# Packing 0/1 rows as byte pairs, an even split of the last rows, and a shared accumulator for the two halves of layer 0

## The reference

```python
# layer 0: keep only edges between nodes of one class, average, mix with h0
a0 = adj * (y @ y.T)
a0 = a0 / maximum(sum(abs(a0), axis=1), 1e-12)
x = layernorm(x + 0.9 * (a0 @ x) + 0.1 * h0)
# layer 1: tanh of the adjacency's own square (one value where there is an edge)
filt = tanh(adj * adj) * (adj > 0)          # then the 350 largest of a row are kept
h2 = tanh(x @ W_proj + b_proj)
x = layernorm(x + relu(filt @ (h2 @ W_gcn) + b_gcn))
```

## Time and profile before

| | |
|---|---|
| median of 3 runs | 467.92 us |
| the profiled execution | 467.66 us |
| its span, from the first to the last instruction | 465.9 us |
| mean granted TensorE clock | 0.986 |
| PE, DVE, ACT, POOL busy | 94%, 81%, 57%, 35% of the span |
| layer 0 with its last blocks | to about 289 us |

### The profile page before, as it was taken

The page is one execution under the profiler, slowest core; times in us unless marked ns, Lnnn a source line. Parts: engine busy times, 40 slices in busy tenths (PEclk is TensorE's granted clock), DMA queues, the critical chain, the costliest instruction groups (busy, mean ns, idle before and its releaser), DMA issues.

```text
span 465.9 us, 15131 instructions
## 1 busy us (share of the span) xinstructions
PE 438.7 (94%) x5104; PEld 386.3 (83%) x5104; DVE 377.9 (81%) x1359; ACT 263.5 (57%) x355; POOL 161.5 (35%) x310
## 2 busy tenths in 40 slices
PE   3659999999999999999999999999999999999994
PEld 2448898888888988888888887888888888888883
DVE  5988999999999999999999976675575575575562
ACT  4997998999999999999999934900000000000000
POOL 3022543455444455554445541221211211211222
PEclk9977999999999999999999999999999999999998
DMA  8999999999999999999999200000000000000000
GB/s 262 411 414 420 419 417 417 415 408 411 409 422 420 422 423 420 424 423 412 417 419 422 60 2 1 13 11 17 17 11 17 17 11 17 17 11 17 17 11 23
DMA packets 25518, 108.50 MB, mean 233 GB/s; under 512 B 5097, under 2 KB 15490, under 8 KB 15490
## 3 DMA queue, kind: packets, MB, share of 16 engines
q1 hardware_dynamic: 25490, 108.14, 57.5%
HBM read 105.57 MB, written 2.56 MB: 232 GB/s over the span
## 4 chain that ended last, share of the span: by engine, by line
PE 75%; DVE 10%; ACT 5%; issue 5%; DMA 2%; POOL 2%; POOLq 0%; DVEq 0%; ACTq 0%; SPq 0%
PE acc L521 64%; PE words L471 6%; DVE a_bits L783 3%; DMA a_rows<-in_adj_dram 2%; PE feat_acc L584 2%; PE proj_acc L595 2%; ACT count_out L685 2%; DVE turned L870 2%; PE xnt_acc L576 1%; ACT count_out L678 1%; ACT x_parts L664 1%; POOL xs L438 1%; ACT count_out L754 1%; DVE z_high L921 1%; ACT count_out L746 1%
## 5 line engine op out<-in xcount | busy, mean ns | idle before, releaser
L521 PE MATMUL acc<-x_parts,turned 128*128 128x257 f16 (+1 forms) x1600 | 195.2, 276 | 3.2 <-DVE turned L870 1.0
L678 ACT ACTIVATE count_out<-a_rows,ones 128x2688 bf16<-128x2688 f32 (+1 forms) x80 | 190.2, 2377 | 0.5 <-DMA a_rows<-in_adj_dram 0.2
L521 PEld LDWEIGHTS acc<-x_parts,turned 128*128 128x128 fp8e4 (+1 forms) x1600 | 154.4, 98 | 28.9 <-issue 3.8
L521 PE MATMUL acc<-f_parts,turned 128*128 128x256 f16 (+1 forms) x1560 | 171.6, 273 | 0.8 <-DVE turned L870 0.8
L521 PEld LDWEIGHTS acc<-f_parts,turned 128*128 128x128 fp8e4 (+1 forms) x1560 | 152.0, 98 | 19.3 <-issue 1.3
L783 DVE TENSOR_SCALAR a_bits<-a_rows 128x2688 bf16<-128x2688 f32 (+1 forms) x80 | 116.7, 1459 | 2.7 <-DMA a_rows<-in_adj_dram 2.3
L421 POOL TENSOR_TENSOR var_eps<-mean_var,consts 128x1 f32<-128x1 f32 x80 | 18.6, 232 | 266.1 <-DVE mean_var L1077 139.7
L870 DVE TENSOR_SCALAR turned<-a_words 128x320 uint16 (+1 forms) x305 | 66.9, 233 | 53.2 <-PE acc L521 52.8
L424 POOL TENSOR_TENSOR rstd<-var_eps,consts 128x1 f32<-128x1 f32 x80 | 86.5, 1081 | 6.3
L870 DVE TENSOR_SCALAR turned<-same_class 128x320 uint16<-128x320 uint16 x313 | 71.3, 254 | 0.1
L471 PEld LDWEIGHTS words<-pack,a_bits 128*128 128x128 bf16 (+1 forms) x1600 | 51.3, 97 | 9.7 <-DVE a_bits L783 7.8
(11 more groups left out here) (111 smaller groups left out, 288.3 us busy)
## 6 DMA issues: line engine op xcount, KB each, us to landing
a_rows<-in_adj_dram SPq DMA_DIRECT2D x39, 1344.0 KB, 7.8
a_rows<-in_adj_dram SPq DMA_DIRECT2D x39, 1156.0 KB, 8.3
out_dram<-xn SPq DMA_DIRECT2D x39, 64.0 KB, 1.5
h_rows<-in_L_gnn_h_dram SPq DMA_DIRECT2D x19, 128.0 KB, 8.1
xs<-in_x_dram SPq DMA_DIRECT2D x3, 640.0 KB, 10.0
xs<-in_x_dram SPq DMA_DIRECT2D x1, 512.0 KB, 10.3
y_nat<-in_L_gnn_y_dram SPq DMA_DIRECT2D x1, 304.0 KB, 3.6
a_rows<-in_adj_dram SPq DMA_DIRECT2D x1, 84.0 KB
```

What stands on the lines that cost most here:

```text
L521: mm = pe.matmul(acc[par][0:m, 0:cols], bits, parts[:, b, 0:cols], start=first and b == blocks[0], stop=last and b == blocks[-1])
L678: act.activation(count_out[0:m, 0:w], a_rows[par][h][0:m, 0:w], ACT.Relu, bias=ones[0:m, 0:1], scale=-HUGE, accum_out=col).then_inc(s_coun ...
```

## The change

Three things are changed together.

- A block's cast writes bytes, 0x3C for a zero and 0x3D for a one. Two neighbouring bytes are read as one f16 weight, whose value is linear in both bits. A packing product so covers 128 pairs of columns: 20 products of 17 columns (16 of powers of two up to 128, one for the count) in place of 40 of 9. ACT takes the offset away and scales by 1024 (`Relu` with a bias), after which a 16-bit word holds 8 rows of two columns. `unpack` makes 8 instructions of 320 elements as before, and `multiply_blocks` reads its weights at every second byte.
- The rows are cut into 38 full blocks and two of 68 rows (the even and the odd rows of the last 136). All loads by pairs begin at row 0 and the halves are 2560 and 2440 columns wide. The words of the two short blocks are copied by three instructions each.
- In layer 0 the product of 257 columns becomes one of 128 (high half) and one of 129 (low half and ones) with the same weights, both added into the same 128 columns of `acc`; `add_high` and `add_low` become one `add_rows`.

The labels' packing at the start follows the new layout (10 turns become 5, 50 products of 256 columns become 25 of 512), and the last check weighs rows differently, in one more instruction. The diff, cut:

```diff
-BITS = 16
+BITS = 8
...
-    FULL = N // P
-    TAIL = N - FULL * P
-    NB = FULL + 1
+    FULL = N // (2 * P) * 2
+    TAIL = (N - FULL * P) // 2
+    NB = FULL + 2
+    COLS = NB // 2
...
+        if isinstance(b, int) and b >= FULL:
+            return a[FULL * P:N, cols].rearrange("(p e) c -> e p c", e=2)[par]
+        v = a[0:FULL * P, cols].rearrange("(s p e) c -> e s p c", p=P, e=2)[par]
...
-        a_bits = [sb(f"a_bits{h}", [P, HB * P], BF16) for h in range(2)]
+        a_bits = [sb(f"a_bits{h}", [P, HB * P], U8) for h in range(2)]
...
-                for b in range(h * HB, HB if h == 0 else NB):
-                    c, d = column(b) - HALF[h].start, spacing(b)
+                for b in range(h * HC, h * HC + HC):
+                    c = (b - h * HC) * P
                     mm = pe.matmul(words[par][:, b * PITCH:b * PITCH + WORDS + 1],
-                                   a_bits[h][0:m, c:c + (P - 1) * d + 1:d], pack[0:m, :], start=True, stop=True)
+                                   a_bits[h][0:m, :].bitcast(F16)[:, c:c + P], pack[0:m, :], start=True, stop=True)
...
             def multiply_blocks(n, par, m, parts, blocks, first=False, last=False):
-                cols = PARTS if parts is x_parts else 2 * F
                 for b in blocks:
-                    bits = turned_at(n, par)[:, b, :].bitcast(F8)[:, 0:m]
-                    mm = pe.matmul(acc[par][0:m, 0:cols], bits, parts[:, b, 0:cols],
-                                   start=first and b == blocks[0], stop=last and b == blocks[-1])
+                    bits = turned_at(n, par)[:, b // 2, :].bitcast(F8)[:, b % 2:2 * m:2]
+                    begin, end = first and b == blocks[0], last and b == blocks[-1]
+                    if parts is f_parts:
+                        mm = pe.matmul(acc[par][0:m, 0:2 * F], bits, parts[:, b, :], start=begin, stop=end)
+                    else:
+                        if not begin:
+                            pe.matmul(acc[par][0:m, 0:F], bits, parts[:, b, 0:F], start=False, stop=False)
+                        mm = pe.matmul(acc[par][0:m, 0:F + 1], bits, parts[:, b, F:PARTS], start=begin, stop=end)
+                        if begin:
+                            pe.matmul(acc[par][0:m, 0:F], bits, parts[:, b, 0:F], start=False, stop=False)
...
+                        act.activation(to[:, :, 0:WORDS + 1], of[:, :, 0:WORDS + 1], ACT.Relu, bias=less_full, scale=UNIT)\
+                            .then_inc(s_words, 1)
...
-                dve.tensor_scalar(a_bits[h][0:m, 0:w], a_rows[par][h][0:m, 0:w], 1.0, None,
-                                  ALU.is_equal).then_inc(s_bits, 1)
+                dve.tensor_scalar(a_bits[h][0:m, 0:w], a_rows[par][h][0:m, 0:w], 1.0, float(ZERO_BYTE),
+                                  ALU.is_equal, ALU.add).then_inc(s_bits, 1)
...
-            def add_high(n, par, m):
+            def add_rows(n, par, m):
                 dve.wait_ge(s_inverse, n + 1)
                 dve.wait_ge(s_xh, n + 1)
-                dve.scalar_tensor_tensor(z_high[0:m, :], acc[par][0:m, 0:F], rs[0:m, 1:2],
-                                         xh[par][0:m, :], ALU.mult, ALU.add).then_inc(s_zhigh, 1)
-
-            def add_low(n, par, m):
-                dve.wait_ge(s_zhigh, n + 1)
                 if not isinstance(n, int) or n >= 2:
                     dve.wait_ge(s_xn, n - 1)
-                dve.scalar_tensor_tensor(z[par][0:m, :], acc[par][0:m, F:2 * F], rs[0:m, 1:2],
-                                         z_high[0:m, :], ALU.mult, ALU.add).then_inc(s_z, 1)
+                dve.scalar_tensor_tensor(z[par][0:m, :], acc[par][0:m, 0:F], rs[0:m, 1:2],
+                                         xh[par][0:m, :], ALU.mult, ALU.add).then_inc(s_z, 1)
```

More of the change, by code:

```diff
@@ L77, in rows_in, with steps @@
     def rows_in(a, b, par, pair, cols):
[L79 to L83, removed]
-        if isinstance(b, int):
[L85 to L99, removed]
+        if isinstance(b, int) and b >= FULL:
+            return a[FULL * P:N, cols].rearrange("(p e) c -> e p c", e=2)[par]
+        v = a[0:FULL * P, cols].rearrange("(s p e) c -> e s p c", p=P, e=2)[par]
+        if isinstance(b, int):
+            return v[pair]
+        return v[bass.ds(pair, 1), :, :].rearrange("a p c -> p (a c)")
+    def steps(eng, step, lag, after={}, first=4):
+        first = max(first, lag + 2 + lag % 2)
         for t in range(first):
@@ L103, in steps @@
                 after[t]()
-        with eng.Fori((first - 1) // 2, (FULL - 1) // 2) as i:
+        with eng.Fori(first // 2, FULL // 2) as i:
+            step(i * 2, 0, i)
             step(i * 2 + 1, 1, i)
-            step(i * 2 + 2, 0, i + 1)
         for t in range(FULL, NB + lag):
@@ L121, in steps4 @@
             step(t, t % 2, t // 2, 0, t)
-        count = (FULL - first) // 4
-        with eng.Fori(0, count) as i:
+        with eng.Fori(0, (FULL - first) // 4) as i:
             for c in range(first, first + 4):
                 step(i * 4 + c, c % 2, i * 2 + c // 2, i, c)
-        for t in range(first + count * 4, NB + lag):
+        assert (FULL - first) % 4 == 0 and first % 2 == 0
+        for t in range(FULL, NB + lag):
             step(t, t % 2, t // 2, 0, t)
@@ L222, in packed_path @@
         GRAM_W = PART * WORDS
[L223 removed]
+        GRAMS = TILES
         EARLY_GRAMS = 3 * GRAMS
@@ new lines, in _ @@
+            pool.affine_select(out=pack[:, WORDS:WORDS + 1], in_=pack[:, WORDS:WORDS + 1],
+                               compare_op=ALU.not_equal, fill=1.0, base=-(P - 1), pattern=[[-1, 1]],
+                               channel_multiplier=1).then_inc(s_pack, 1)
+            for bit in range(BITS):
+                pool.wait_ge(s_pack, bit + 3)
+                pool.affine_select(out=pack[:, 0:WORDS], in_=pack[:, 0:WORDS], compare_op=ALU.not_equal,
+                                   fill=float(1 << bit), base=-bit * WORDS, pattern=[[-1, WORDS]],
+                                   channel_multiplier=1).then_inc(s_pack, 1)
@@ L397, in _, with zeros_as_words @@
+            def zeros_as_words(rows):
+                return -ZERO_VALUE * sum(1 << bit for bit in range(BITS) if rows > bit)
+            whole, rest = divmod(TAIL, WORDS)
+            for c, v in ((less_full, zeros_as_words(BITS)), (less_long, zeros_as_words(whole + 1)),
+                         (less_short, zeros_as_words(whole)), (less_count, -ZERO_VALUE * 2 * TAIL)):
+                pool.memset(c, v).then_inc(s_const, 1)
             pool.memset(ident[:, :], 0.0).then_inc(s_const, 1)
-            for c, v in ((neg_half, -0.5), (ln_eps, LN_EPS), (alpha, ALPHA)):
+            for c, v in ((neg_half, -0.5), (ln_eps, LN_EPS), (alpha, ALPHA), (row_weight, 2.0)):
@@ L865, in unpack @@
                     dve.wait_ge(s_acc, n - 1)
-                last = HALF_BITS if m == P else 1
-                for bit in range(lo // 2, min(hi // 2, last)):
+                last = -(-m // WORDS)
+                for bit in range(lo, min(hi, last)):
                     shift = ONE_BIT - bit
```

266 lines of the change are left out of this document (129 added, 137 removed).

## The result

The changed kernel takes 483.94 us (median of 4 runs, 483.25 to 489.14) where the kernel before takes 467.86 (467.48 to 468.11): a ratio of 1.0368, with a 95% interval of 1.0296 to 1.0441. It is slower, by 16.1 us. The prediction said 481.3 us, within 476 to 491. The profiled execution took 483.54 us with a span of 481.7, 15.8 longer than before. The highest of the four, 489.14 us, had a mean granted clock of 0.964 where the other three had 0.971; it has no trace, so what made it longer is open. It widens the interval.

A forecast was written before the change was run, and what follows sets the result against it. PE and DMA were taken as equally long in layer 0, with DMA's end deciding. Later drain 11.5, clock 2.1 and checks -0.2 sum to +13.4 us on the median 467.92: 481.3 us, range 476 to 491.

The forecast's parts named there:

- The engines of 68 rows: Row loads of the last two blocks: 68 rows use four DMA engines, the same four for both, 12.9 us a block.
- The last landing: 278.6 us: End of layer 0's row loads: 25.7 us for both short blocks from 252.9, where the kernel before cast at 267.08.
- After the last landing: End of layer 0: 2.24 us of DVE work, then 10.7 us for the last two blocks' products, ending at 291.6.
- The clock: 2.1 us, bounds 0 and 5: PE, idle while late rows come, drops to the low clock for some 4.3 us of products, losing 2.1 us.
- PE's step, 6.20 - 0.49 + 0.21 = 5.92 us: PE in a layer 0 step: packing saves 0.49 us, the split product adds 0.21, leaving it under DMA's 6.21.
- The split term 0.21: Layer 0 product on PE: a pair of 128-column products takes 117 ns, 5.4 more than one of 257; +0.21 us per step.
- Rival 2: A 128-column product in layer 0 costs more than 62 ns: 490 us at 65 ns, 530 at 78; chance 0.09.
- The cast keeps its rate: DVE's cast in layer 0, now writing bytes with two operations, stays at 0.58 ns an element: no change.
- rival 3: DVE's cast loses its double rate, making its step 8.9 us: +100 us, near 580; chance 0.03.
- DMA as a floor of 6.21 us: Layer 0's row transfer takes 6.21 us a step, as long as PE before, and the change can't lower it.
- Checks and layer 1: -0.2 us: Last count on ACT, holding PE in early layer 1, gets 0 to 0.8 us shorter, one more check costs 0.2; layer 1 unchanged.
- Rival 1, rows spread over all engines: 466.5: The last two blocks' 68 rows use all engines, land before their casts are due, and the drain gains 1.4 us; chance 0.11.

The follow-up runs named there:

- kernel 1: The changed kernel with each row load of the two 68-row blocks cut into 64 and 4 rows: 469.41 us, 1.0035 of the kernel before.
- kernel 2: The changed kernel with each row load of the two 68-row blocks cut into 34 and 34 rows: 502.77 us.
- kernel 3: The changed kernel with 24 unused products ahead of each packing of a short block (96 in all), to keep TensorE busy: 480.89 us.
- kernel 7: kernel 1 with only the first half of each half block's columns loaded from block 4 to 37, engine work unchanged: 456.27 us.
- kernel 5: The kernel before with only layer 0's product split into 128 and 129 columns and one addition for two: 473.11 us.
- kernel 8: The kernel before with only the first half of each half block's columns loaded from block 4 to 37: 467.79 us.

## Why the prediction was right, point by point

- *The engines of 68 rows.* Right. The mechanism that set the sign was read from 2401 small packets; the count after (2293), kernel 1 and kernel 2 all show it.
- *The last landing: 278.6 us.* The mechanism was right and the size off. The last cast came at 282.37, 3.8 later. The term took 26.4 GB/s for each engine, a sixteenth of 423; in the five windows of 5 us from 255 to 280 four of them gave 96, 98, 91, 100 and 86 GB/s, 94 on the mean. Less the h0 rows in it that is 22.8 each, and 2.72 MB take 29.8 us in place of 25.7. The start was off too, the other way: DMA moves 356 GB/s from 249 to 250 us, then 189, 145 and 89 in the next three, so the other twelve engines had run dry by 252, 1 to 2 us before the 252.9 that the prediction took. And the four don't end together, as the prediction took it: in the four windows of 1 us from 278 to 282 the share is 0.16, 0.11, 0.11 and 0.06 of 16 engines, two to three of them at first and one at the end, so the slowest sets the landing. Why four engines run below a sixteenth each is not settled; two of them kept it in kernel 2 (26.6).
- *After the last landing.* 2.24 us to the first product were taken, 1.92 measured (282.37 to 284.29). The products of two blocks, taken as 10.7 us, took 13.14, of which 3.0 are the clock: 10.1.
- *The clock: 2.1 us, bounds 0 and 5.* The mechanism was right, the size too small. The products of block 38 ran at half clock from 284.3 to 290.3, 3.0 us lost, and kernel 3 gave back 3.05. The low stretch lasted 6 us, not 4.3 as at the start of the program.
- *PE's step, 6.20 - 0.49 + 0.21 = 5.92 us.* Nearly right: 58.3 ns a product against 58.5 taken, and 5.965 us a step in kernel 7, where PE is full with DVE and ACT. The split term 0.21 shows as 0.17 in kernel 5. Rival 2 (over 62 ns) is refuted, and the 81 ns that the prediction set beside it do not hold for this stream: 257 columns in two products cost hardly more than in one, also with the weights read at every second byte.
- *The cast keeps its rate.* Right, 0.58 ns an element; rival 3 is refuted.
- *DMA as a floor of 6.21 us.* Right for the changed kernel, 6.216. The prediction took PE and DMA as equally long before; kernel 8 shows that the engines set the step of the kernel before, 6.25 us with full and with half loads against a transfer of 6.21. So the change did shorten layer 0's steps, by 0.03 us of the 0.286 that its engines saved. The rest went into waiting for the transfer.
- *Checks and layer 1: -0.2 us.* Mis-sized, and beyond its bound of 0.8. The stall of 0.84 us is gone: the products of early layer 1 follow each other in the chain. The time from 297.43 to the end of the span is 184.3 us, before 185.8 from 280.07 on: 1.6 less, where the sum had 0.2. Besides the 0.84, the last features of layer 0 take 0.5 less (8.17 us from there to the long run of layer 1 products at 305.60, before 8.66 to 288.73) and what follows the last products 0.1 less; neither was put in the sum, and the cause of the 0.5 is open.
- *Rival 1, rows spread over all engines: 466.5.* The kernel that spreads them over 16 engines took 469.4, because the rival left out that partitions 0 to 63 take only half the rate. With both mended it is 464.4, and 462.5 to 463.8 as a whole kernel. (The 3.3 us a block that the prediction gave for 16 engines is 3.2: 1.36 MB at 423 GB/s.)

The sum: 15.8 us of span against 13.4 predicted. Of the 2.4 between the two, 3.4 are the later first product and 0.9 the clock; the faster products take 0.6 off and what lies behind them 1.4 (the parts are rounded). That the sum came closer than its largest error is luck: two terms were too high where two were too low. What decided sign and size, few engines for 68 rows, was foreseen.

## What to carry to other kernels

Before blocks are cut anew, work out for each transfer on how many DMA engines its rows divide and which partitions it writes: here a load of 68 rows ran at 94 GB/s, one of 64 rows in partitions 0 to 63 at 202 to 206, and the same 64 rows in every second partition at 331 over 5 us. Ask of each engine's saving what the next floor is: 0.286 us a step of engine time was worth 0.03 with the transfer at 6.216 us. And a change that is slower as a whole may hold a faster kernel: the same packing with its last rows spread takes 462.5 to 462.9 us, 1.1 to 1.2% under the kernel before.

## What the runs showed of the hardware that was not expected

- 16 busy DMA engines moved 202 to 206 GB/s into partitions 0 to 63, and 331 over the same 5 us (374 and 364 in its fullest two) into every second partition of all 128.
- Four engines gave 22.8 GB/s each, two 26.6, sixteen 26.4, and the four did not end together. Why is open.
- The DMA share is 1.01 in layer 0 of kernels with 406 as of those with 426 GB/s: a full share does not say that the transfer sets the step.
- A shift by 32 bytes of the buffers, and all tensors behind them, changed the rate of all row loads between 422 and 426 GB/s, and the time by 1.2 to 1.4 us, in both directions.
- Idle stretches of TensorE of a few us at a time cost 3.0 us of clock in the work behind it, and 96 products whose results are not used gave it back.
